# Router weights asked for earlier, and a new order of the work where attention passes into the experts

## The chip, the cores and the metric

One core of a Trainium2 chip runs the kernel. Its five engines (TensorE or PE for matmuls, VectorE or DVE, ScalarE or ACT, GpSimd or POOL, and SyncE or SP, which here only issues DMAs) each run their own list of instructions in order and meet at semaphores. The metric is the device time of one execution in microseconds (us).

## What is computed

16 batches of 256 tokens of width 256 go through a gated cross attention and a mixture of 8 experts, of which each token takes 2. Cut to what matters:

```python
q = layernorm(x)                                # per batch [256, 256]
K, V, Q = q @ wk, q @ wv, ctx @ wq              # the reference calls them so
attn = softmax(Q @ K.T, axis=2)
x = x + tanh(g_xattn) * (attn @ V)
xt = layernorm(x).reshape(4096, 256)
scores = xt @ Wg.T                              # 8 experts
top_scores, top_idx = top_k(scores, 2)
y_e = (silu(xt @ W1[e].T) * (xt @ W2[e].T)) @ W3[e].T     # hidden width 704
out = sum over the two chosen e of top_scores * y_e
x = x + tanh(g_ffn) * out
```

The function is called with the context as the query side: `_L0_xattn_ref(ctx_1024, _layernorm(x), ...)`; in the kernel x gives the rows of the result and the context gives what they attend to.

## The kernel before

**Attention, 16 steps.** Step n works on batch n. SP loads x(n) and the context. PE turns x (`turn_x`), multiplies (`product`, L823) and turns the probabilities (`turn_probs`); ACT takes the exponents (`exponents`, L673) and copies out of PSUM; DVE takes maxima, moments and the residual (`residual`, L1161 to L1169). The residual of batch n is made in step n + 1, after `values(n)` on PE. In the same steps the expert weights are cut in two f16 parts. ACT makes the high part (`high3`, L679, and the scaled copy at L725), DVE the low part (`lo12`, L1074, and `lo3`, L1081), with a scale worked out from sums of squares (L874, L1054, L1056). DVE takes the first moments of x(n + 2) ahead of the scale of step n (`first_moments`, L1100).

**Routing.** For a batch m whose residual is done, DVE takes `second_moments` (L1178), POOL makes the power -0.5 of the variance (`deviations`, L549 to L552, or `second_deviations`, L560 to L562), DVE chooses experts (`choose`, L1190 to L1214), PE counts ranks (`rank`, L837), DVE makes `slots` (L1138 to L1147), and POOL scatters the rows in four indirect DMAs (`scatter`, L572) into `rows_by_expert`. `AT_STEP` routes batches 0 to 9 in the steps, `AT_PAIR` batches 10 to 15 in pairs 0 to 5 of the expert stage. For batches 0 to 9 the normed rows are made on POOL (`low_rows`, L582 to L591), for the others on DVE and ACT (`centre_rows` L1112, `high_rows` L1122, `norm_rows` L658).

**Experts.** 32 pairs of tiles of 128 gathered rows, then 7 single tiles. For pair i, SP fetches rows (L502), PE turns them (`turn_gathered`, L866), ACT copies (`copy_turned`, L700), PE multiplies the gate part (36 matmuls, L946) and the upper part (30), ACT takes the silu (`gate`, L745 and L747), DVE multiplies (`mixed` L1380, `combined` L1386), ACT and DVE cut the result in two parts (`high` L756, `low` L1402 and L1403), PE makes the output (`to_output`, L978) one pair later, ACT scales it (L769), and POOL adds it into `out` (`add_rows`, L613). `units` (L1060 to L1228) prepares scales that `gate` needs.

**The order around the change.** All order is written out by hand: each engine runs its own function with a loop over steps and then one over pairs, and every instruction behind a wait stands with it. At the start, SP asks for wq, wk, context 0, x(0), wv and the first expert weights, and ACT asks for the router weights `wg_s` once wk is there. PE first sums the router weights (L884), then turns x(0). At step 15 ACT copies the first gathered rows before its high part, and PE turns them before `values(14)`. In pair 0 PE turns the last probabilities, makes `values(15)` and waits for the residual of batch 15 before the rank of batch 10; DVE makes that residual after choosing batch 10. POOL makes the power for batch 10 after the four scatters of batch 8.

## Time and profile before

| what | value |
|---|---|
| median of 3 runs | 597.12 us (595.77 to 597.38) |
| profiled execution, its own time | 590.55 us |
| its span, first to last instruction | 588.80 us |
| PE busy | 561.5 us, 95% |
| DVE, ACT, POOL busy | 322.2, 312.8, 290.4 us |
| mean granted clock of PE | 0.988 |
| attention steps and their seam to the experts | 0 to about 176 us |
| expert pairs and tiles | about 160 to 589 us |

A row of the timeline gives the start in us, the duration, the engine, the line, the operation with what it writes and reads, how many instructions are merged, and in brackets how long the engine had been idle and who released it. PEld is the load of weights into PE, SPq and ACTq are DMA issues. A granted clock of 1.00 is 2.4 GHz and 0.50 is 1.2 GHz.

### The profile page before, as it was taken

To read this page: it belongs to the slowest core of one execution; us is meant where nothing else is said; L and a number is where in the kernel's file an instruction comes from. 1 tells how busy PE (TensorE), PEld (TensorE's weight loads), DVE (VectorE), ACT (ScalarE), POOL (GpSimd) and SP (SyncE) were. 2 spreads that over 40 slices of the span, in tenths; PEclk is the share of its full clock that TensorE was granted. 3 is DMA by queue.
4 is the path that set the end of the run, shared out by engine and by line. 5 is a ranking of instruction groups with operands and counts; after the bars stand their busy time and mean duration, and the time that the engine had idled before them with its cause. 6 is when DMAs were issued, how large, how long until landed. Compare 5 with 4: busy or idle time off the path is not lost.

```text
span 588.8 us, 14558 instructions
## 1 busy us (share of the span) xinstructions
PE 561.5 (95%) x4641; PEld 489.8 (83%) x4641; DVE 322.2 (55%) x908; ACT 312.8 (53%) x438; POOL 290.4 (49%) x262
## 2 busy tenths in 40 slices
PE   6998999999779999899999999999999999999995
PEld 5787887787668999789988988988898899898883
DVE  2499898899877776843433343343334334333332
ACT  2787988788654555353534444354453444434442
POOL 3039898988984766643243333324323233333323
PEclk8999999999898999999999999999999999999999
DMA  7647879786413344532323323322232332322322
GB/s 252 191 156 213 256 258 291 210 278 182 159 69 122 77 85 114 162 65 49 56 39 47 66 40 47 54 51 41 47 65 39 47 63 42 47 40 43 53 35 27
DMA packets 52371, 61.49 MB, mean 104 GB/s; under 512 B 7632, under 2 KB 46160, under 8 KB 52304
## 3 DMA queue, kind: packets, MB, share of 16 engines
q1 hardware_dynamic: 34096, 38.14, 21.8%
q0 software_dynamic: 13296, 18.23, 18.2%
q10 hardware_dynamic: 4912, 4.20, 2.1%
q8 instruction: 45, 0.74, 0.5%
q14 instruction: 22, 0.18, 0.1%
HBM read 36.90 MB, written 23.66 MB: 103 GB/s over the span
## 4 chain that ended last, share of the span: by engine, by line
PE 71%; POOL 19%; issue 4%; DVE 2%; DMA 2%; ACT 1%; POOLq 0%; SPq 0%; DVEq 0%
PE psum L946 38%; PE psum L978 22%; POOL rows_by_expert L572 7%; POOL arena L582 5%; PE psum L955 4%; PE psum L866 3%; POOL rstd L552 2%; POOL xn2r L591 2%; PE psum L823 1%; POOL xn2r L588 1%; DMA wg_s<-in_WgT 1%; POOL var_eps L550 1%; PE psum L964 1%; DMA arena<-in_wkT 1%; POOL var_eps L549 0%
## 5 line engine op out<-in xcount | busy, mean ns | idle before, releaser
L613 POOL DMA_INDIRECT out<-w_in,id_s x71 | 129.5, 1823 | 235.0 <-ACT w_in L769 117.7
L946 PE MATMUL psum<-arena,w_hi 128*128 128x256 f16 x1408 | 213.2, 274 | 1.7 <-issue 1.7
L946 PEld LDWEIGHTS psum<-arena,w_hi 128*128 x1408 | 138.4, 98 | 19.1 <-issue 2.0
L946 PE MATMUL psum<-arena,w_lo 128*128 128x256 f16 x704 | 135.4, 274 | 0.0
L700 ACT ACTIVATE arena<-psum 128x1024 f16<-128x1024 f16 (+1 forms) x39 | 36.9, 947 | 106.0 <-PE psum L866 106.0
L1386 DVE SCALAR_TENSOR_TENSOR arena<-psum,h_unit,arena 128x1280 f32<-128x1280 f32 x32 | 49.6, 1551 | 64.7 <-PE psum L946 64.6
L572 POOL DMA_INDIRECT rows_by_expert<-xn2r,slot_i x64 | 72.1, 1127 | 18.2 <-issue 17.6
L946 PEld LDWEIGHTS psum<-arena,w_lo 128*128 x704 | 69.3, 98 | 8.4
L823 PE MATMUL psum<-arena 128*128 128x264 f32 x256 | 65.3, 401 | 3.5 <-DVE place L1138 3.2
L745 ACT ACTIVATE arena<-psum,w_unscale 64x256 f32<-64x256 f32 x32 | 15.0, 467 | 86.6 <-PE psum L946 86.6
L978 PE MATMUL psum<-w_hi,arena 128*128 x396 | 59.0, 273 | 1.0 <-ACT arena L759 1.0
L1380 DVE SCALAR_TENSOR_TENSOR arena<-psum,h_unit,arena 64x256 f32<-64x256 f32 x32 | 15.7, 490 | 77.2 <-ACT arena L747 77.0
L823 PEld LDWEIGHTS psum<-arena 128*128 128x128 f32 x256 | 47.3, 194 | 12.1 <-DVE halves L1054 4.0
L978 PE MATMUL psum<-w_hi,w_in 128*128 x385 | 57.3, 273 | 0.0
L747 ACT ACTIVATE arena<-psum,w_unscale 128x1280 f32<-128x1280 f32 x32 | 42.5, 1327 | 0.4
L978 PEld LDWEIGHTS psum<-w_hi,arena 128*128 128x128 f16 x396 | 37.8, 98 | 5.5 <-issue 1.2
L769 ACT ACTIVATE w_in<-psum,wsum 128x256 f32<-128x256 f32 x71 | 33.1, 467 | 14.5 <-PE psum L978 14.5
L978 PEld LDWEIGHTS psum<-w_hi,w_in 128*128 128x128 f16 x385 | 36.8, 98 | 4.1
L978 PE MATMUL psum<-w_lo,arena 128*128 x216 | 33.5, 272 | 0.0
L978 PE MATMUL psum<-w_lo,w_in 128*128 x210 | 32.5, 273 | 0.0
L823 PE MATMUL psum<-wv_s,arena 128*128 128x264 f32 x128 | 31.2, 387 | 0.3 <-ACT wv_s L711 0.3
L823 PE MATMUL psum<-arena,qk 128*128 128x256 f32 x128 | 30.9, 385 | 0.0
(195 smaller groups left out, 860.8 us busy)
## 6 DMA issues: line engine op xcount, KB each, us to landing
xa<-rows_by_expert SPq DMA_DIRECT2D x71, 136.0 KB, 2.2
w_in<-in_W1T SPq DMA_DIRECT2D x8, 704.0 KB, 5.4
w_in<-in_W2T SPq DMA_DIRECT2D x8, 640.0 KB, 5.0
w_in<-in_W3T SPq DMA_DIRECT2D x8, 640.0 KB, 5.9
arena<-in_ctxT SPq DMA_DIRECT2D x16, 256.0 KB, 6.1
xa<-in_x SPq DMA_DIRECT2D x16, 256.0 KB, 6.3
out<-xa ACTq DMA_DIRECT2D x16, 256.0 KB, 4.7
out<-w_in,id_s POOLq DMA_INDIRECT x71, 4.5
```

Of the source, the lines that this page charges most:

```text
L572: pool.indirect_dma_start(out=xs[:, :], out_offset=bass.IndirectOffsetOnAxis(ap=slot_i[:, k, col:col + 1], axis=0), in_=xn2r[:, m % ROWS, ...
L582: ins = pool.tensor_scalar(xn2f[:, t, :], xa[:, x_at(m) + t, :], mv2[:, m % 2, t, 0:1], rstd[:, half_of(m), t:t + 1], ALU.subtract, ALU.mult)
L613: pool.indirect_dma_start(out=out[:, :], out_offset=bass.IndirectOffsetOnAxis(ap=id_s[:, t8:t8 + 1], axis=0), in_=y_s[:, t8 % 4, :], in_of ...
L700: act.activation(xg_t[:, k, :, :, 0:n], xt_ps[:, :, :, 0:n], ACT.Copy).then_inc(s_xgt, 1)
L747: act.activation(act_g[:, 0:KF * N2], g_ps, ACT.Silu, scale=w_unscale[:, 0, bass.ds(expert[u], 1)].bitcast(F32)).then_inc(s_silu, 1)
L769: act.activation(y_s[:, t8 % 4, :], y_ps[t8 % 2], ACT.Copy, scale=wsum[:, t8:t8 + 1]).then_inc(s_y_copied, 1)
L823: ins = pe.matmul(dst[:, t, :], left[:, c, t * P:(t + 1) * P], right[:, c, :], start=(c == 0), stop=(c == 1))
L866: ins = pe.transpose(xt_ps[:, h, c, half * P:(half + 1) * P], xg[:, k, half, at:at + P // 2].bitcast(F16), ident16[:])
L946: ins = pe.matmul(flat_ps[:, j * N2:(j + 1) * N2], w12[w_part][:, c, bass.ds(e * (2 * H) + j * P, P)], xg_t[:, k, x_part, c, :], start=(q ...
L955: ins = pe.matmul(dst, xg_t[:, k, x_part, c, 0:P], w12[w_part][:, c, bass.ds(e * (2 * H) + at, n)], start=(q == 0 and c == 0), stop=(q == ...
L978: ins = pe.matmul(y_ps[t8 % 2], hid_p[k4 % 2][:, c * n + h * P:c * n + (h + 1) * P], w3[w_part][:, r, bass.ds(e * D, D)], start=(q == 0), ...
L1386: dve.scalar_tensor_tensor(out=hid[:, 0:KF * N2], in0=u_ps, scalar=h_unit[:, 0, bass.ds(e, 1)].bitcast(F32), in1=act_g[:, 0:KF * N2], op0= ...
```

## The change

It has three parts. At the start, SP asks for the router weights as its third request; ACT waits for wq instead of wk and asks only for the two gates. At step 15, ACT copies the first gathered rows after its high parts and exponents, and makes the high part of the last W3 there; PE makes `values(14)` first, then turns the gathered rows and the last probabilities. In step 15 and pair 0, DVE makes `units` after the residual of batch 14, `mixed` and the residual of batch 15 ahead of the choice of batch 10, and the low part of the last W3 after `combined(0)`; POOL makes the power of batch 10 ahead of the scatters of batch 8, and that of batch 11 ahead of those of batch 9. No instruction is added or removed.

```diff
             sp.dma_start(wk_t, ...).then_inc(s_wk, 16)
+            sp.dma_start(wg_s[:], WgT.rearrange("(c p) e -> p c e", p=P)).then_inc(s_wg_in, 16)
             load_ctx(0)
...
                 if n in AT_STEP:
                     low_rows(AT_STEP[n])
+                if n == B - 1:
+                    second_deviations(IN_STEPS)
                 if n - 1 in AT_STEP:
                     scatter(AT_STEP[n - 1])
-            second_deviations(IN_STEPS)
...
             for i in range(SLOTS + 1):
+                if i + 1 in AT_PAIR:
+                    second_deviations(AT_PAIR[i + 1])
                 if i == 0:
                     scatter(IN_STEPS - 1)
-                if i + 1 in AT_PAIR:
-                    second_deviations(AT_PAIR[i + 1])
...
-            act.wait_ge(s_wk, 16)
-            act.dma_start(wg_s[:], ...).then_inc(s_wg_in, 16)
+            act.wait_ge(s_wq, 16)
...
                 if live(n - 2):
                     store_rows(n - 2)
-                if n == B - 1:
-                    copy_turned(0, 0)
                 if live(n):
...
-                if live(n) and k == 1 and n < B - 1:
+                if live(n) and k == 1:
                     high3(e)
+                if n == B - 1:
+                    copy_turned(0, 0)
...
                 if at == 0:
-                    high3(E - 1)
+                    copy_probs(B - 1)
                     act.activation(silu_first[:], tanh_g[:], ACT.Silu)
-                    copy_probs(B - 1)
                     act.wait_ge(s_unit, 1)
...
                 if k == 1:
                     weight_sum3(n // 2)
+                if live(n - 1):
+                    values(n - 1)
                 if n == B - 1:
                     pe.wait_ge(s_pt_copied, B - 1)
                     turn_gathered(0, 0, 0)
-                if live(n - 1):
-                    values(n - 1)
+                    turn_probs(B - 1)
...
                         if at == 0:
                             to_hidden(range(4), expert[u], k)
-                            turn_probs(B - 1)
                             pe.wait_ge(s_v_copied, B)
...
-                if n == B - 1:
-                    units()
                 if n in AT_STEP:
                     choose(AT_STEP[n])
...
+            units()
             second_moments(IN_STEPS)
-            lo3(E - 1)
...
+                if at == 0:
+                    mixed(i, expert[u])
+                    residual(B - 1)
                 if m is not None:
                     centre_rows(m)
                     high_rows(m)
                     choose(m)
                 if on(i):
-                    if pair(i):
+                    if pair(i) and at > 0:
                         mixed(i, expert[u])
                     weights_and_rows(i, j, k4, expert[u])
+                    combined(i, expert[u])
                     if at == 0:
-                        residual(B - 1)
-                    combined(i, expert[u])
+                        lo3(E - 1)
                     low(i, k)
```

## Rows read from the trace of the kernel before

**Rows 1.** The page, part 1: busy time, share of the span, instructions.
```profile
PE 561.5 (95%) x4641; PEld 489.8 (83%) x4641; DVE 322.2 (55%) x908; ACT 312.8 (53%) x438; POOL 290.4 (49%) x262
```
**Rows 2.** Chain that ended last, in order of time: start, us, what.
```profile
4.97 5.88 DMA wg_s<-in_WgT
...
176.51 9.94 PE psum L946 x66
...
188.81 3.93 PE psum L946 x36
...
245.85 1.70 issue
```
**Rows 3.** Timeline of the start, 0 to 24 us.
```profile
10.98 0.84 PE L884 MATMUL psum<-wg_s,ones_f 128*128 128x8 f32 x4 [3.29 <-DMA wg_s<-in_WgT]
...
17.94 0.75 DVE L1100 BATCH_NORM_STATS2 stats<-xa 128x6 f32<-128x256 f32 x2 [2.65 <-DMA xa<-in_x]
...
19.63 1.46 ACT L725 ACTIVATE w_hi<-w_in,w_scale 128x1408 f16<-128x1408 f32 x1
...
21.96 0.56 ACT L673 ACTIVATE arena<-psum,nbias,rstd 128x256 f32<-128x256 f32 x1 [0.87 <-DVE nbias L1157]
```
**Rows 4.** Timeline of the seam, 150 to 180 us: PE and ACT.
```profile
157.92 1.01 PE L866 MATMUL psum<-ident,xa 128*128 128x128 f16 x8 [3.01 <-DMA xa<-rows_by_expert]
...
158.73 3.29 PE L823 MATMUL psum<-arena 128*128 128x264 f32 x8
...
158.97 1.02 ACT L700 ACTIVATE arena<-psum 128x1024 f16<-128x1024 f16 x1 [4.49 <-PE psum L866]
...
162.33 1.57 ACT L679 ACTIVATE w_hi<-w_in,w_scale 128x1536 f16<-128x1536 f32 x1
...
176.29 0.19 PE L837 MATMUL psum<-mask,before 128*128 128x16 bf16 x1 [3.90 <-DVE xa L1169]
```
**Rows 5.** Stretches: us, busy of PE, PEld, DVE, ACT, POOL, clock, DMA share, GB/s.
```profile
11.00:13.00 2.00, 2.00 (x11) 2.00 (x12) 0.24 (x2) 0.19 (x1) 0.00 (x0) 0.54 0.59 192
...
178.00:180.00 2.00, 2.00 (x11) 1.40 (x10) 0.75 (x2) 1.21 (x1) 0.00 (x0) 0.50 0.93 298
...
190.00:300.00 110.00, 108.31 (x1036) 97.26 (x1034) 64.87 (x192) 52.02 (x66) 59.48 (x45) 1.00 0.39 84
```
**Rows 6.** DMA queues, 5 to 11 us: packets, MB, share of 16 engines.
```profile
q1 hardware_dynamic: 1475, 1.79, 89.7%
q10 hardware_dynamic: 392, 0.01, 3.6%
```
**Rows 7.** Timeline of the seam, 150 to 186 us: DVE.
```profile
156.23 0.40 DVE L1060 TENSOR_SCALAR w_unscale<-halves 128x16 int32<-128x16 int32 x2
...
157.33 1.22 DVE L1228 SCALAR_TENSOR_TENSOR unscale_y<-unscale_y,tanh_g,h_unit 128x8 f32<-128x8 f32 x1
...
161.38 2.02 DVE L1074 SCALAR_TENSOR_TENSOR w_lo<-w_in,w_scale,w_hi 128x704 f16<-128x704 f32 x2 [1.30 <-ACT w_hi L725]
...
164.57 0.74 DVE L1178 BATCH_NORM_STATS2 stats<-xa 128x6 f32<-128x256 f32 x2
...
171.79 0.16 DVE L1112 SCALAR_TENSOR_TENSOR shift<-mv,rstd 128x2 f32<-128x2 f32 x1 [3.00 <-POOL rstd L562]
...
174.17 0.49 DVE L1380 SCALAR_TENSOR_TENSOR arena<-psum,h_unit,arena 64x256 f32<-64x256 f32 x1
...
176.15 1.54 DVE L1386 SCALAR_TENSOR_TENSOR arena<-psum,h_unit,arena 128x1280 f32<-128x1280 f32 x1
...
179.24 0.42 DVE L1402 TENSOR_TENSOR arena<-arena 64x256 f16<-64x256 f32 x1 [1.55 <-ACT arena L756]
179.67 1.49 DVE L1403 TENSOR_TENSOR arena<-arena 128x1280 f16<-128x1280 f32 x1
...
185.11 0.36 DVE L1210 SCALAR_TENSOR_TENSOR xn2r<-arena,rstd,mask 128x8 f32<-128x8 f32 x2
```
**Rows 8.** Waits of DVE, 176 to 255 us: us in total, times, longest.
```profile
DVE arena L1386 <- PE psum L946: 5.9, 5, 2.4
```

More of the change, by code:

```diff
@@ L634, in _ @@
         def _(act):
-            act.wait_ge(s_wk, 16)
-            act.dma_start(wg_s[:], WgT.rearrange("(c p) e -> p c e", p=P)).then_inc(s_wg_in, 16)
+            act.wait_ge(s_wq, 16)
             with nc.allow_non_contiguous_dma(reason="one gate to every partition"):
```

## Prediction, made before the changed kernel was run

> **What bounds the kernel now.** I read the page first: TensorE (PE) is busy 95% of the span [rows 1]. That is an average over three stages, so the second view is the chain of waits in order of time. From 176.51 us on it is PE alone, pair after pair, with one gap of 1.70 us at 245.85 [rows 2]. Work that the change leaves as it is fills that stage, so the stage gets shorter only if it begins earlier. The question is how much earlier PE gets into it, and whether a wait grows inside it. The third view is the timeline of the two places where the change acts: the start, and the seam from 154 to 177 us between the last attention batches and the first expert pairs. At the start PE sits idle 3.29 us until the router weights land at about 10.9 us [rows 3]. At the seam it idles 3.01 us until the first gathered rows land (157.9), and 3.90 us until the residual of batch 15 is written (176.3) [rows 4]. The fourth view is the table by stretch: the granted clock is 0.54 in 11 to 13 us and 0.50 in 178 to 180, its lower level of 1.2 GHz, right after the idles of 3.29 and 3.90 us, and 1.00 from 190 to 300 [rows 5]. At 158 the slow values after the third idle show the same. What that costs is seen in the chain: 66 matmuls from 176.51 took 9.94 us, while 36 of the same kind took 3.93 us at the upper level (2.4 GHz) [rows 2], so 66 would take 7.2.
>
> Below, times are those of the profile of before; I first work out the seam as if it began at its old time, then add the start.
>
> **Part 1, router weights third on SP's queue.** The request moves from 4.97 us on ACT's queue to about 1.8 us, behind two loads. The sum L884 could then start when the q-k product ends, 10.98 less the idle 3.29, so at 7.7: PE leads by 3.3 us, and with no idle there is no reason for the fall of the clock either. But the next end is near. At batch 0 DVE takes the moments of x(2) before it makes the scale that ACT waits for, and it waited 2.65 us for x(2) to land at 17.9 [rows 3]. Those moments take until about 19.0 whatever PE does (0.75 and a short second instruction); the scale's two small instructions follow in some 0.35, so ACT's first high part (1.46 us, at 19.63) can start at 19.35 and end at 20.8. There the exponents of batch 0 start, which before came at 21.96 because the scores came late [rows 3]. So **1.1 us** of the 3.3 reach ACT, which is the dense engine of the next steps. All later loads are issued on semaphores of this work, so I let 1.1 us pass through to the seam.
> What it costs: one more issue on SP ahead of the first context, x(0) and value weights. The 256 rows of 32 bytes are small packets: in 5 to 11 us the queue of ACT moved 392 of them in 3.6% of 16 engines' 6 us, which is 9 ns each, where the 1475 packets of SP's queue took 58 ns each [rows 6]. So 256 take 256 x 9 / 16 = 0.14 us, and did so before as well. If each were as dear as a large one it would be 0.93 us, x(2) would land that much later and the 1.1 would be 0.2. I take 1.1, since the 9 ns are of the same transfer.
> The Trainium skill (DMA: Bandwidth & Descriptors, "Issuing engines are not separate DMA queues") says that the queues of all issuing engines end on the same 16 DMA engines and that spreading requests only saves issue time. By that rule the queue itself gives nothing, and only the 3.1 us earlier request counts; the landing 5.9 us after the issue, behind seven loads, agrees [rows 2]. The same page (Specifications) says that transfers below 512 bytes are slowed by a read-modify-write; by it the upper cost would be the likely one; the 9 ns of this trace speak against it.
>
> **Part 2, order at batch 15 on PE and ACT.** Before, ACT stood 4.49 us on the turn of gathered rows (L700 at 158.97) in front of the high part of batch 15, and PE stood in front of the values of batch 14, which then ran 3.29 us at the low clock [rows 4]. After: PE runs the values at once, 154.9 to 156.9 (3.29 at the low clock; between half of it, 1.65, and that; I take 2.0, as four such take 1.0), and idles about 1 us to 157.9, not 3. Then the turn (8 transposes) and the probabilities of batch 15 (4) at the upper level: done at 159.1. ACT: high part 154.75 to 156.2 (1.46, as in [rows 3]), exponents (two of 0.56 there) to 157.3, high part of W3 1.57 to 158.9 [rows 4], then the copy of the turned rows 158.9 to 159.9. That is the same end as before (158.97 + 1.02), so ACT's 4.1 us of work go into its wait at no cost. PE's first expert matmul starts at 159.9 instead of 161.64, where it stood behind the slow values.
> The gate part of pair 0 is 36 matmuls, 3.93: 164.0 (0.1 more for the rank). The values of batch 15 (two halves of about 1.0) end at 166.1 at the earliest.
>
> **Part 3, order on DVE.** Five spans between rows of DVE [rows 7] give the pieces: units 156.23 to 158.55 = 2.32; choice of batch 9, 158.55 to 160.08 (161.38 less its wait of 1.30) = 1.53; low part and residual 14, 161.38 to 164.57 = 3.19; centre, high rows and choice of batch 10, 171.79 to 174.17 = 2.38; mixed, weights and residual 15, 174.17 to 176.15 = 1.98. After: choice from 156.2 to 157.8, low part and residual 14 to 160.95 (its high part was ready at 156.2), units to 163.3, moments of batch 10 (about 0.95) to 164.2, slots 0.5, moments 11 to 165.7. ACT's gate starts at 164.05, when PE is done, and takes 1.8; units at 163.3 are in time by 0.7 us, which is their cover. Then mixed and residual 15 end at **167.6**, where before they ended at 176.15. PE no longer waits for them: its upper part of pair 0, 30 matmuls at 3.93 / 36, runs 166.1 to 169.5.
> Late next is the choice of batch 10, which now stands behind the residual: 167.6 + 2.38 = 170.0. The rank of batch 10 on PE waits for it, and so does the product u times gate (L1386), at 170.4 instead of 176.15. PE turns pair 1 by 170.1, ACT copies it in 1.02, and pair 1 starts at 171.2, not 176.49: **5.3 us**. PE's idle pieces are now 0.9, 0.8, 1.0 us; the 1.70 us of [rows 2] did not lower the clock [rows 5]. So 66 matmuls take 7.2, not 9.94, and PE leads by 8.0 at 178.4.
> Then DVE is late. The low part of W3 (1.8 us; L679 on ACT took 1.57 for the same tile) is put into the 1.55 us that DVE waits for ACT's high part [rows 7], so it costs 0.3 there: pair 0's low part ends at 175.7 (before 179.67 + 1.49 = 181.16). From that end to the weighted rows of batch 11 it took 185.11 + 0.36 - 181.16 = 4.3 [rows 7]: 180.0. PE reaches the rank of batch 11 at 178.9 and waits 1.1. Pair 2 starts about 1.9 after the rank, at 182.0, against 188.7 in [rows 2]: **6.5 us** (0.2 off for small issues). From there DVE waits for PE again in every pair (five times, 5.9 us in all, before this product [rows 8]), so it doesn't fall behind; the 1.70 at 245.85 stands behind DVE's planning of the later slots, which starts from PE's own product, so it stays.
>
> **Part 4, POOL.** The power of batch 10 goes in front of four scatters. DVE waited 3.00 us for it until 171.79 [rows 7]. Now POOL reaches it at 164.4 and the moments are there at 164.2, so it is ready at 165.4, and 167.6 needs it: 2 us of cover. The scatters of batches 8 and 9 move back 1.1 each (two powers of that size ahead of them); batch 9's end at about 177.3, as before. Queued behind are the power of batch 12 (needed at 188), scatter 10 and the first add, which needs pair 0's product only at 182.6. SP's gathers of pair 8 need all scatters 60 us later. So nothing here.
>
> **Sum.** 1.1 + 6.5 = 7.6 us. The profiled execution took 590.55 (span 588.80) and would take 583.0. The median of the runs shown is 597.12, 6.6 above the profiled one; I carry the difference over whole: 597.12 - 7.6 = **589.5**. As PE's clock differs from run to run, an error in that carry is likelier than one in the profile.
>
> **Rivals.**
> A, the whole wait at the start counts: 3.3 us and about 1.6 of low clock pass on, total 11.4, 585.7. For it: the weights' transfer is 5.88 us of the chain. Against: x(2), above. 0.05.
> B, the start gives nothing, since x(2) lands later: total 6.5, or 5.6 if everything behind slides: 590.6 to 591.5. 0.17.
> C, the clock falls once more. Three idles of 1 us lie within 14 us. At half rate from 171 on, pair 1 takes 9.9 again, but the 1.1 of waiting for DVE goes: 2.7 - 1.1 = 1.6 lost, or 3.3 if it happens at 158 too (less what DVE hides): 591 to 593. The Trainium skill (TensorE: Matmul & The Clock Gate, Part 1) says the clock follows how busy PE has been, so several short idles could add up to one long; by that rule C would be the forecast, at 591.1; the trace has no such cluster. 0.15.
> D, DVE takes the place of the waits: units or the values of batch 15 come later than I think and the choice of batch 10 holds rank, product and pair 1. For each microsecond one is lost; at 4 it is 593.5, at 7 nothing is left. 0.06.
> E, slower: PE stays at 1.2 GHz from 158 through 185, since its work is spread thinner, never idle long but never dense. Before, it was low for about 10 us of that stretch; 17 more cost 8.4 us, against 3.8 saved idle and 1.1: 597.12 + 3.5 = 600.6. It turns slower once the low time exceeds the old by 10 us. Against: 66 dense matmuls alone brought the level back. 0.03.
> F, the change doesn't do what it says: POOL's chain, unchanged up to 164, sets the seam, and PE's idle only moves from the residual to the choice of batch 10. Then some clock and 1 us are gained: 595 to 597. Against: the power of batch 10 leaves the queue of scatters. 0.05.
>
> **How the numbers follow.** The forecast has 0.49. The range is 586.5 to 594.0: below it A, above it E, F and the end of D; the lower end is the forecast with the 1.1 of waiting gone and x(2) 2 us earlier. Faster by over 0.3% (1.8 us, about what a measurement can tell from none): 0.91. Within: 0.05. Slower: 0.04.
>
> **What would show it.** In the profile after: L884 at about 7.7; the first L673 at 20.9; clock 1.00 in 11 to 13; the first L946 near 158.8 (159.9 less 1.1); no wait of PE on L1169; pair 1 at 170.1, and a wait of about 1 us at the second L837 of the expert phase, released by DVE's L1210. The exponents at 21 or later say B; clock 0.50 past 158 says C; a long wait of PE on DVE's choice says D or F.

## The result: faster by 1 to 4.5 us, where 7.6 were predicted

| comparison | before | changed | ratio, 95% interval |
|---|---|---|---|
| first | 596.43 us (594.88 to 602.7, 19 runs) | 594.4 us (592.24 to 598.21, 19 runs) | 0.9957 [0.9937, 0.9977] |
| second (`after_again`) | 590.52 us (24 runs) | 586.0 us (7 runs) | 0.9933 [0.991, 0.9957] |
| third (`after_third`) | 596.42 us (33 runs) | 595.34 us (10 runs) | 0.9969 [0.9943, 0.9995] |

The changed kernel is faster. The 594.4 us lie just above the range (586.5 to 594.0), and the gain in that comparison is 2.0 to 2.6 us. Medians are taken over all runs of a kernel and ratios over its fast runs alone (one run of `before_again` took 2064 us), so the two can differ a little. The kernel before itself took 590 us in two comparisons and 596 in four; a section below shows what differs between these. The readings of the change are taken from traces of the first kind, where ACT has no pause of unknown cause: `before_again` (the kernel before, span 589.4), the trace shown ahead of the prediction (span 588.80), and `after_again` (the changed kernel, span 584.0, its own time 585.78). Between these spans the gain is 4.8 or 5.4 us, between the medians of that comparison 4.5.

Profile of the changed kernel (`after_again`), the page, part 1: busy time, share, instructions. PE is busy 559.6 us, not 561.5; with the shorter span its share went up by a point, and so did those of PEld and ACT [rows 1].

```profile
span 584.0 us, 14559 instructions
PE 559.6 (96%) x4641; PEld 488.3 (84%) x4641; DVE 322.8 (55%) x908; ACT 312.9 (54%) x438; POOL 290.7 (50%) x262
```

Its start, rows of the timeline; they answer [rows 3].

```profile
7.79 0.51 PE L884 MATMUL psum<-wg_s,ones_f 128*128 128x8 f32 x4
...
12.14 1.38 ACT L688 ACTIVATE w_hi<-w_in 128x1408 bf16<-128x1408 f32 x1 [2.71 <-DMA w_in<-in_W1T]
...
14.45 3.89 PE L823 MATMUL psum<-wv_s,arena 128*128 128x264 f32 x8 [2.70 <-ACT wv_s L712]
...
19.21 0.75 DVE L1100 BATCH_NORM_STATS2 stats<-xa 128x6 f32<-128x256 f32 x2 [4.76 <-DMA xa<-in_x]
...
20.52 1.47 ACT L724 ACTIVATE w_hi<-w_in,w_scale 128x1408 f16<-128x1408 f32 x1 [1.44 <-DVE w_scale L1056]
...
22.14 0.56 ACT L674 ACTIVATE arena<-psum,nbias,rstd 128x256 f32<-128x256 f32 x1 [0.16 <-DVE nbias L1157]
```

PE's wait of 3.29 us for the router weights is gone. In its place PE waits 2.70 us at 14.45 for the value weights from ACT, and ACT had waited 2.71 us for the first expert weights (W1) to land at 12.1. PE's granted clock is 0.50 from 13.1 to 19.9 us. DVE waits 4.76 us for x(2), which lands at 19.2 instead of 17.9, and ACT's first exponents start at 22.14 instead of 21.96.

PE at the seam, rows of the timeline of `after_again`; they answer [rows 4] and the chain in [rows 2].

```profile
158.06 0.61 PE L866 MATMUL psum<-ident,xa 128*128 128x128 f16 x8 [1.05 <-DMA xa<-rows_by_expert]
...
160.12 0.61 PE L947 MATMUL psum<-arena,w_hi 128*128 128x256 f16 x4 [1.01 <-ACT arena L701]
...
166.53 1.13 PE L823 MATMUL psum<-arena 128*128 128x264 f32 x4 [1.38 <-DVE place L1138]
...
171.97 0.17 PE L837 MATMUL psum<-mask,before 128*128 128x16 bf16 x1 [0.58 <-DVE xn2r L1210]
...
172.69 0.61 PE L947 MATMUL psum<-arena,w_hi 128*128 128x256 f16 x4 [0.53 <-ACT arena L701]
...
181.66 0.18 PE L837 MATMUL psum<-mask,before 128*128 128x16 bf16 x1 [1.15 <-DVE xn2r L1210]
...
183.89 0.60 PE L947 MATMUL psum<-arena,w_hi 128*128 128x256 f16 x4
```

The idles of 3.01 and 3.90 us have become 1.05 and 0.58. A new one of 1.38 stands at 166.5, behind DVE. The granted clock stays up; table by stretch (us; busy time of PE, PEld, DVE, ACT, POOL; clock; DMA share; GB/s), against [rows 5]:

```profile
11.00:13.00 2.00, 0.75 (x7) 0.66 (x6) 0.00 (x0) 0.86 (x1) 0.00 (x0) 1.00 0.96 329
178.00:180.00 2.00, 2.00 (x21) 1.80 (x20) 1.97 (x9) 1.20 (x2) 1.48 (x4) 1.00 0.24 85
```

DVE and POOL at the seam, `after_again`, rows of the timeline of each (against [rows 7]):

```profile
157.06 0.45 DVE L1197 TENSOR_TENSOR hot<-idx,iota_e 128x32 f32<-128x32 uint32 x1
...
157.76 1.01 DVE L1206 TENSOR_TENSOR seen<-seen,mask 128x8 bf16<-128x8 bf16 x1
...
163.05 1.00 DVE L1227 TENSOR_TENSOR unscale_y<-w_unscale 128x8 f32<-128x8 f32 x1
...
166.22 0.17 DVE L1138 TENSOR_TENSOR place<-psum,region_of 128x16 f32<-128x16 f32 x1 [0.95 <-issue]
...
172.09 1.54 DVE L1384 SCALAR_TENSOR_TENSOR arena<-psum,h_unit,arena 128x1280 f32<-128x1280 f32 x1
...
156.86 0.61 POOL L589 CAST xn2r<-arena 128x512 f16<-128x512 f32 x1
...
157.57 1.18 POOL L592 TENSOR_TENSOR xn2r<-arena,xn2r 128x512 f16<-128x512 f32 x1
...
162.88 1.15 POOL L592 TENSOR_TENSOR xn2r<-arena,xn2r 128x512 f16<-128x512 f32 x1
```

Three instructions of DVE that take 0.16 to 0.19 us elsewhere took 0.45, 1.01 and 1.00, and each ended within 0.04 us of the end of a POOL instruction that had begun before it: 157.51 against 157.47, 158.77 against 158.75, 164.05 against 164.03. And DVE idles 0.95 us from 165.3 on with no releaser. From 150 us to the rank of batch 11 at 181.66, the chain of waits of this trace is DVE's alone; the idle is in it as these pieces (start, us, what; L397 loads the number of an expert into a register):

```profile
165.10 0.16 DVEq L395
165.26 0.72 issue
165.98 0.19 DVEq L397
```

### The profile page after: what moved, and what is told of

Its sections match the earlier page's. It is cut to its first block, busy times and chain, and to the rows that moved or that the text cites. A ratio compares the mean times of both kernels' runs of the same rounds, so it can differ in the third digit from the quotient of the medians.

```text
span 596.5 us, 14559 instructions
## 1 busy us (share of the span) xinstructions
PE 564.6 (95%) x4641; PEld 489.2 (82%) x4641; DVE 322.6 (54%) x908; ACT 312.9 (52%) x438; POOL 292.2 (49%) x262
## 3 DMA queue, kind: packets, MB, share of 16 engines
q0 software_dynamic: 13296, 18.23, 17.9%
## 4 chain that ended last, share of the span: by engine, by line
PE 72%; DVE 15%; issue 4%; ACT 4%; SPq 2%; DMA 1%; another core or an unknown queue 1%; POOLq 0%; ACTq 0%; DVEq 0%
PE psum L947 38%; PE psum L979 22%; PE psum L956 4%; PE psum L823 4%; DVE w_lo L1074 3%; PE psum L866 3%; DVE xa L1169 1%; DMA xa<-in_x 1%; DVE stats L1100 1%; DVE w_lo L1081 1%; DVE stats L1178 1%; DVE nmax L1153 1%; PE psum L965 1%; ACT w_hi L688 1%
## 5 line engine op out<-in xcount | busy, mean ns | idle before, releaser
L947 PE MATMUL psum<-arena,w_hi 128*128 128x256 f16 x1408 | 215.0, 276 | 7.5 <-ACT arena L701 6.6
L947 PEld LDWEIGHTS psum<-arena,w_hi 128*128 x1408 | 138.9, 99 | 26.1 <-issue 8.7
L947 PE MATMUL psum<-arena,w_lo 128*128 128x256 f16 x704 | 135.9, 275 | 0.7 <-issue 0.7
L1384 DVE SCALAR_TENSOR_TENSOR arena<-psum,h_unit,arena 128x1280 f32<-128x1280 f32 x32 | 49.6, 1551 | 69.2 <-PE psum L947 66.8
L573 POOL DMA_INDIRECT rows_by_expert<-xn2r,slot_i x64 | 74.1, 1157 | 18.2 <-issue 17.9
L947 PEld LDWEIGHTS psum<-arena,w_lo 128*128 x704 | 69.5, 99 | 9.8 <-issue 1.2
L823 PE MATMUL psum<-arena 128*128 128x264 f32 x256 | 64.1, 396 | 3.8 <-DVE place L1138 3.5
L823 PEld LDWEIGHTS psum<-arena 128*128 128x128 f32 x256 | 46.3, 190 | 12.1 <-DVE halves L1054 3.5
L724 ACT ACTIVATE w_hi<-w_in,w_scale 128x1408 f16<-128x1408 f32 x16 | 23.5, 1469 | 15.7 <-DVE w_scale L1056 15.6
```

The costliest lines, as they stand in the source:

```text
L573: pool.indirect_dma_start(out=xs[:, :], out_offset=bass.IndirectOffsetOnAxis(ap=slot_i[:, k, col:col + 1], axis=0), in_=xn2r[:, m % ROWS, ...
L724: act.activation(w12[0][:, :, n * H:(n + 1) * H], w12_in[:, k], ACT.Copy, scale=w_scale[:, 0:1].bitcast(F32)).then_inc(s_hi12, 1)
L823: ins = pe.matmul(dst[:, t, :], left[:, c, t * P:(t + 1) * P], right[:, c, :], start=(c == 0), stop=(c == 1))
L947: ins = pe.matmul(flat_ps[:, j * N2:(j + 1) * N2], w12[w_part][:, c, bass.ds(e * (2 * H) + j * P, P)], xg_t[:, k, x_part, c, :], start=(q ...
L1384: dve.scalar_tensor_tensor(out=hid[:, 0:KF * N2], in0=u_ps, scalar=h_unit[:, 0, bass.ds(e, 1)].bitcast(F32), in1=act_g[:, 0:KF * N2], op0= ...
```

## Experiments

To compare traces whose start differs, I use two figures: the time at which ACT's first exponents start (**start**), and the time from DVE's maximum over the scores of batch 15 (L1153) to the first product of u and gate (L1386, in the changed kernel L1384) (**seam**). Kernel before: seam 21.01 and 20.70; changed: 16.75.

### Start and seam apart

`start_only` takes this from the change and nothing else:

```diff
             sp.dma_start(wk_t, wkT.rearrange("(c p) d -> p c d", p=P)).then_inc(s_wk, 16)
+            sp.dma_start(wg_s[:], WgT.rearrange("(c p) e -> p c e", p=P)).then_inc(s_wg_in, 16)
             load_ctx(0)
...
-            act.wait_ge(s_wk, 16)
-            act.dma_start(wg_s[:], WgT.rearrange("(c p) e -> p c e", p=P)).then_inc(s_wg_in, 16)
+            act.wait_ge(s_wq, 16)
```

`seam_only` is the rest of the change. `before_again` and `after_again` are the two kernels once more.

> The kernel before, unchanged, for a second trace beside the others of this group. Its first trace spanned 588.8 us, while its runs lie at 595 to 600. If that trace was an unusually undisturbed execution, this one spans 592 to 597 and shows idle pieces of 2 to 6 us in the expert pairs that the first did not have; if those pieces in the trace of the changed kernel belong to the change, this one has none of them. Ratio to the kernel before: 1.000.

> The changed kernel, unchanged, for a second trace. Its first trace had ACT idle for 4.7 us before the copy of the turned rows of pair 2 (186.9 us), and PE idle 3.3 us behind that, then a lower clock. If this belongs to the new order, it is there again at the same instruction and pair 2 starts near 188; if it is a disturbance of that one execution, pair 2 starts near 183.5 (about 5 us ahead of the kernel before). Ratio 0.995 to 0.997.

> Part 1 alone: the router weights are asked for third on SP's queue, everything else as before. Theory 1 (the load of x(2) ends the wait, and it lands later than before): exponents of batch 0 within 0.3 us of before, ratio 1.000 +- 0.002. Theory 2 (my prediction's 1.1 us, hidden in the trace by chance): exponents at 20.9 us, ratio 0.998. Theory 3 (the small rows delay the value weights, as seen in one trace, where they landed at 10.4 instead of 7.3 us): the value weights land after 10 us again.

> Parts 2 to 4 alone: the router weights are asked for by ACT as before, the order of step 15 and of pair 0 is the new one. Theory 1 (the gain of the change comes from the seam alone): the same time as the whole change, ratio 0.995 to 0.997, the product of pair 0 near 172.4 us. Theory 2 (the seam's gain is what I predicted, 6.5 us, and the start takes part of it back): ratio 0.989 to 0.992.

| kernel | median | ratio | x(2) at DVE | start | seam |
|---|---|---|---|---|---|
| before_again | 590.68 | 0.9995 [0.9979, 1.0011] | 17.25 | 23.67 | 20.70 |
| start_only | 589.77 | 0.9992 [0.9978, 1.0005] | 19.65 | 22.53 | 20.68 |
| seam_only | 587.17 | 0.995 [0.993, 0.9969] | 18.25 | 22.02 | 16.76 |
| after_again | 586.0 | 0.9933 [0.991, 0.9957] | 19.21 | 22.14 | 16.75 |

The start alone can't be told from no change; the seam alone is nearly the whole. The pause of 4.7 us in the first trace of the changed kernel is not in `after_again`, where pair 2 starts at 183.89; so it does not come with the new order by itself. In `before_again` PE's granted clock was at its lower level from 10.7 to 17.5 us and its exponents came at 23.67. `start_only` and `after_again` show the lower level too, from 13.1 to 19.9, about the wait for ACT's value weights (3.40 and 2.70 us). Of the nine traces with the start of the change, six have a low stretch between 13 and 21 us, with one such wait of 2.6 to 3.6 us; in the other three the waiting is split in pieces of 2.2 us and less, and the clock stays at 1.00. So what the earlier weights save of low clock, PE mostly pays a little later.

### What holds the start

> The changed kernel with the router weights asked for by ACT as its very first instruction, not by SP as its third. Theory 1 (the small rows in SP's queue push x(2) back, which landed at 19.1 to 19.7 us in three traces with them and at 17.3 to 18.3 in three without): the sum of the router weights starts at 7.5 to 7.9, x(2) lands by 18.3 and the exponents of batch 0 start at 21.0 to 21.3, 1 us ahead of the changed kernel's 22.1; ratio to the kernel before 0.991 to 0.992. Theory 2 (x(2) is late because all loads share the same bandwidth and PE, being ahead, asks for context 2 sooner): x(2) lands after 19 us again, ratio 0.993.

> The changed kernel with x(2) asked for ahead of the second batch of weights W2 and W3 instead of behind them. Theory 1 (the first exponents now wait for x(2), which lands at 19.0 to 19.7 us in five traces of the changed start): x(2) lands before 15 us, and the exponents of batch 0 start at 20.6 to 21.2 instead of 21.7 to 22.9; median 0.7 to 1.3 us under the changed kernel. Theory 2 (PE's own work and its clock set the first exponents, x(2) is only the last to be seen): still 21.7 or later, median as the changed kernel's or up to 1 us above it, since W2 and W3 land later.

> As combo, but x(2) is asked for behind the second weights, as in the changed kernel. Theory 1 (x(2) holds the start up also when wg is out of SP's queue): x(2) lands at 18.2 to 18.7, first exponents at 20.9 to 21.3, 0.4 to 0.8 us behind combo. Theory 2: no difference to combo.

> The changed kernel with three edits: ACT asks for wg in its first instruction, x(2) is asked for ahead of the second weights, and DVE loads the numbers of the first eight experts behind the low halves of batch 15. Theory 1 (they are three separate waits): x(2) lands by 15 us, the first exponents start at 20.3 to 20.8, the seam takes 15.9 to 16.3; 2.0 to 3.0 us under the changed kernel on the same chip. Theory 2 (PE's work sets the first exponents once x(2) is there, at 21.0): the start gives 1.0 at most, the whole 1.5 to 2.0.

wg_act_first, against the changed kernel:

```diff
-            sp.dma_start(wg_s[:], WgT.rearrange("(c p) e -> p c e", p=P)).then_inc(s_wg_in, 16)
             load_ctx(0)
...
         def _(act):
+            act.dma_start(wg_s[:], WgT.rearrange("(c p) e -> p c e", p=P)).then_inc(s_wg_in, 16)
             act.wait_ge(s_wq, 16)
```

x2_early, against the changed kernel:

```diff
             load_ctx(1)
+            load_x(2)
             load_w12(1)
             load_w3(0)
-            load_x(2)
```

`combo` has both and the early register load (below); `start_combo` is combo without the early x(2). First the rows of x2_early, then of combo (timelines of DVE and ACT):

```profile
15.86 0.75 DVE L1100 BATCH_NORM_STATS2 stats<-xa 128x6 f32<-128x256 f32 x2 [0.46 <-DMA xa<-in_x]
21.04 0.56 ACT L674 ACTIVATE arena<-psum,nbias,rstd 128x256 f32<-128x256 f32 x1 [0.87 <-DVE nbias L1157]
```

```profile
13.89 0.75 DVE L1100 BATCH_NORM_STATS2 stats<-xa 128x6 f32<-128x256 f32 x2 [0.17 <-DMA xa<-in_x]
20.09 0.56 ACT L674 ACTIVATE arena<-psum,nbias,rstd 128x256 f32<-128x256 f32 x1 [0.87 <-DVE nbias L1157]
```

| start as in | first exponents, every trace |
|---|---|
| the kernel before | 21.96, 22.02, 23.61, 23.67 |
| the change | 21.35, 21.71, 21.78, 21.80, 22.14, 22.53, 22.79, 22.87, 22.92 |
| the change, wg by ACT at once (x(2) late) | 21.12, 21.43 |
| the change, x(2) early | 21.04 |
| both | 20.09, 20.39, 20.75, 20.78 |

x2_early had been expected to bring x(2) before 15 us; it was 15.86, but the exponents came where expected. Medians: wg_act_first 584.62 (before 590.11 there), 0.9911 [0.9894, 0.9929]; x2_early 591.27 (before 595.7), 0.9934 [0.9896, 0.9973]. So both waits were real: from the mean of the nine (22.2) the one edit moves the exponents by 0.9 us, the other by 1.2, both together by 1.7. These are figures of the traces; the medians of these comparisons don't tell 1 us apart. The four traces with the start of before have a mean of 22.8, so the change's start is 0.6 ahead on average, with values that overlap. With the change's own start, x(2) was seen by DVE at 18.7 to 19.7 in nine traces; with the start of before, at 17.3 to 18.3 in four. SP's issues of the loads ahead of it took longer (3.06 us for the last two of W3 in `after_again`, 1.33 in the trace of before) and it was issued at 10.7 to 12.4 us in the nine traces, against 8.5 to 10.2 in the four of the old start. In four traces with the router weights in SP's queue PE also waits for the value weights, which land at 9.7 to 11.9 us (theory 3 of start_only); start_only itself does not show that wait. With the router weights asked for by ACT at once x(2) was issued at 10.0 and 10.4, and DVE saw it at 18.45 and 18.75.

The tables by stretch of before_again and of after_again, in that order, 5 to 10 us, show the DMA engines less full in the new start:

```profile
5.00:10.00 5.00, 1.97 (x8) 1.44 (x8) 1.31 (x6) 1.88 (x2) 0.84 (x3) 1.00 0.95 315
```

```profile
5.00:10.00 5.00, 4.77 (x30) 4.17 (x29) 2.52 (x9) 2.25 (x3) 0.98 (x3) 1.00 0.78 274
```

Why they are less full is not settled: the share is 0.83 in wg_act_first as well, where the small packets are not in SP's queue, so these packets alone are not it.

### Which engine's order makes the seam

Each of these leaves the order of one engine, or of PE and ACT, as before, or changes PE and ACT alone. The edits are the pieces of the change's diff for these engines, taken back or taken alone. That of pool_undone, against the changed kernel:

```diff
-                if n == B - 1:
-                    second_deviations(IN_STEPS)
                 if n - 1 in AT_STEP:
                     scatter(AT_STEP[n - 1])
+            second_deviations(IN_STEPS)
...
-                if i + 1 in AT_PAIR:
-                    second_deviations(AT_PAIR[i + 1])
                 if i == 0:
                     scatter(IN_STEPS - 1)
+                if i + 1 in AT_PAIR:
+                    second_deviations(AT_PAIR[i + 1])
```

> The changed kernel with DVE's whole order as before: units ahead of the choice of batch 9, the choice of batch 10 ahead of mixed and the residual of batch 15, the low part of W3 before pair 0. The orders of PE, ACT, POOL and the start are the new ones. Theory 1 (most of the seam's gain is PE no longer waiting for the residual): PE waits 2 us or more for L1169 again, ratio 0.996 to 0.998. Theory 2 (the gain is that of PE's and ACT's order at step 15): ratio 0.993 to 0.994.

> The changed kernel with POOL's part undone: the power for batch 10 after the four scatters of batch 8 again, that for batch 11 after those of batch 9. Theory 1 (this power must be ready when the residual of batch 15 is done, at 169.6): the power is ready at about 171 to 171.8, DVE waits 1.5 to 2.2 us for it, and the time rises by as much, ratio 0.996 to 0.997. Theory 2 (POOL's part has cover and is worth nothing): ratio 0.993.

> The kernel before with only the orders of PE and of ACT at the seam changed (value products ahead of the turn of gathered rows, the turn of the probabilities behind it, ACT's copies and the last squares in the order that this needs); start, DVE and POOL are as before. The time from the scores of batch 15 to the first combined step is 20.7 us in the kernel before, 16.75 in the changed one, 16.69 with DVE's order put back, 17.46 with POOL's put back. Theory 1 (PE's order makes the gain, DVE's order is worth nothing, POOL's 0.7): 17.3 to 17.6 us, so 3.1 to 3.4 us under the kernel before in the median. Theory 2 (each of the two is worth nothing only while the other is there): 18.5 us or more, the gain 2 us or less.

> The changed kernel with the orders of PE and of ACT at the seam as before; start, DVE and POOL are changed. Theory 1 (PE's order makes the gain): PE waits at its first turn of gathered rows about 3 us as before, and the seam takes 19.8 to 20.7 us, of which POOL's part takes at most 0.7; median within 1 us of the kernel before. Theory 2 (the wait of 3.9 us on the last residual is DVE's and POOL's to remove): the seam takes 18 us or less.

| order at the seam | median | before there | ratio | seam |
|---|---|---|---|---|
| all changed (after_again) | 586.0 | 590.52 | 0.9933 [0.991, 0.9957] | 16.75 |
| DVE as before | 585.6 | 590.11 | 0.9917 [0.9897, 0.9936] | 16.69 |
| POOL as before | 585.45 | 590.11 | 0.9929 [0.9909, 0.9948] | 17.46 |
| PE and ACT as before | 593.88 | 595.7 | 0.9952 [0.9917, 0.9986] | 18.12 |
| only PE and ACT changed | 595.79 | 595.7 | 1.0001 [0.9964, 1.0038] | 19.66 |
| nothing changed (before_again) | 590.68 | 590.52 | 0.9995 [0.9979, 1.0011] | 20.70 |

The changed seam takes 16.72 to 16.76 us in the three traces without pauses of ACT (after_again, seam_only, wg_act_first) and 17.2 to 17.4 in the three with them (the first trace, x2_early, after_third). The two rows of PE and ACT are of the second kind, so between them and the others only steps of 1 us and more count; the 0.7 of POOL is between traces of the first kind. The expectations missed more than once. dve_undone was to wait 2 us or more for L1169 or be worth as much as PE's order alone; PE waits 0.92 and the time is that of the change. pool_undone was to rise by 1.5 to 2.2 us; DVE waits 0.56 and the median does not rise. The two rows of PE and ACT came out against theory 1: with these alone it said 17.3 to 17.6, and it is 19.66; with these undone 19.8 to 20.7, and it is 18.12. Theory 2 of pe_act_only holds: the parts are not a sum. Rows of the timeline that say why, of pe_act_only (DVE, PE), where both old waits stand unchanged:

```profile
172.11 0.16 DVE L1111 SCALAR_TENSOR_TENSOR shift<-mv,rstd 128x2 f32<-128x2 f32 x1 [2.99 <-POOL rstd L562]
176.61 0.18 PE L836 MATMUL psum<-mask,before 128*128 128x16 bf16 x1 [3.90 <-DVE xa L1168]
```

of pool_undone (DVE):

```profile
168.72 0.16 DVE L1111 SCALAR_TENSOR_TENSOR shift<-mv,rstd 128x2 f32<-128x2 f32 x1 [0.56 <-POOL rstd L563]
```

of dve_undone (PE, DVE):

```profile
173.03 0.18 PE L837 MATMUL psum<-mask,before 128*128 128x16 bf16 x1 [0.92 <-DVE xa L1169]
158.39 1.23 DVE L1228 SCALAR_TENSOR_TENSOR unscale_y<-unscale_y,tanh_g,h_unit 128x8 f32<-128x8 f32 x1
```

The wait of 3.90 us for the residual comes from DVE's wait of 3 us for POOL's power of batch 10. Two edits remove that: POOL makes the power before its scatters, or DVE does the residual before it asks for the power. With PE and ACT changed, DVE's edit alone takes the seam from 19.66 to 17.46 and POOL's alone to 16.69; POOL's on top of DVE's adds 0.7, DVE's on top of POOL's nothing. And the new order of PE and ACT is worth 1.0 alone and up to 1.4 on top of the others.

Why is DVE's order worth nothing once POOL's is changed? Add its pieces up, from the instruction behind the last w_scale (L1056) to the first product: 15.69 us in after_again (156.40 to 172.09), 15.60 in dve_undone (157.29 to 172.89). The change takes the low half of W3 out (1.70), exposes the register load that it had hidden (0.95), and puts choice and units at moments at which POOL's instructions stretch them more: 2.64 + 1.99 = 4.63 against 1.54 + 2.25 = 3.79, so 0.84. 0.95 + 0.84 - 1.70 = +0.09.

### The two costs on DVE, each taken away

`regs_early` loads the eight numbers behind the low halves of batch 15, `pool_quiet` lets POOL compute the low rows of batches 8 and 9 on 8 of 256 columns; it leaves out the others, so its result is not the function's and it serves for the timing alone.

regs_early:

```diff
                 if n == B - 1:
                     lo12(n)
+                    held = [dve.alloc_register(f"expert_{u}") for u in range(UNROLL)]
+                    expert = {}
+                    dve.wait_ge(s_map, 1)
+                    take_experts(dve, held, expert, 0, UNROLL)
                 if live(n - 1):
                     residual(n - 1)
...
-            held = [dve.alloc_register(f"expert_{u}") for u in range(UNROLL)]
-            expert = {}
...
-            dve.wait_ge(s_map, 1)
-            over_slots(dve, moe_step, lambda i, n: take_experts(dve, held, expert, i, n))
+            over_slots(dve, moe_step, lambda i, n: take_experts(dve, held, expert, i, n) if i > 0 else None)
```

pool_quiet, the first of its three instructions (the cast and the subtraction are cut in the same way):

```diff
+                w = 8 if m in (8, 9) else D
                 for t in range(KT):
-                    ins = pool.tensor_scalar(xn2f[:, t, :], xa[:, x_at(m) + t, :], mv2[:, m % 2, t, 0:1],
+                    ins = pool.tensor_scalar(xn2f[:, t, 0:w], xa[:, x_at(m) + t, 0:w], mv2[:, m % 2, t, 0:1],
```

> The changed kernel with DVE's load of the experts of pairs 0 to 7 into registers put right behind the low part of batch 15, where DVE is busy, and not between the moments of batch 10 and the slots of batch 9. Theory 1 (the idle 0.95 us before L1138 in the trace of the changed kernel is this load, and PE's 1.38 us wait for L1138 is mostly it): the idle piece is gone, PE's wait for L1138 is 0.4 to 0.5, the product of pair 0 starts 0.9 us earlier at about 171.2, ratio 0.9915 to 0.992. Theory 2 (DVE waits there for PE's rank of batch 9): nothing moves, ratio 0.993.

> The changed kernel in which POOL computes the low rows of batches 8 and 9 on 8 of 256 columns (the other columns keep older values), so that POOL's operations of 0.6 to 3.3 us beside the choice of batch 9 and the units are nearly gone. Theory 1 (DVE's small operations are stretched by POOL's that run beside them): the choice of batch 9 takes 1.5 to 1.6 us instead of 2.64, the units 1.1 to 1.3 instead of 1.99, PE's wait of 1.38 us for the places is gone, and the seam takes 15.0 to 15.5 us instead of 16.75; median 1.2 to 1.7 us under the changed kernel. Theory 2 (the stretch has to do with the operations themselves or with DMA): choice 2.6, units 2.0, time as the changed kernel's.

regs_early: 583.42 us, 0.990 [0.9882, 0.9918], seam 15.91. PE's wait for the places is 0.38 instead of 1.38 (timeline, PE):

```profile
163.71 1.13 PE L823 MATMUL psum<-arena 128*128 128x264 f32 x4 [0.38 <-DVE place L1138]
```

pool_quiet: 590.5 us (before 595.7), 0.9877 [0.9813, 0.994], seam 16.38; timeline, DVE:

```profile
156.56 0.19 DVE L1198 TENSOR_TENSOR hot<-idx,iota_e 128x32 f32<-128x32 uint32 x1
...
157.00 0.17 DVE L1207 TENSOR_TENSOR seen<-seen,mask 128x8 bf16<-128x8 bf16 x1
...
160.82 0.17 DVE L1228 TENSOR_TENSOR unscale_y<-w_unscale 128x8 f32<-128x8 f32 x1
...
164.11 0.17 DVE L1139 TENSOR_TENSOR place<-psum,region_of 128x16 f32<-128x16 f32 x1 [1.92 <-PE psum L839]
```

The stretch is POOL's: all three instructions are back at 0.17 to 0.19, the choice takes 1.54 (155.89 to 157.43; expected 1.5 to 1.6) and the units 0.77. That is 2.3 us less for DVE, but the seam became only 0.4 shorter: DVE now waits 1.92 for PE, whose gathered rows came 3.9 us after the scores instead of 2.7. The expected 15.0 to 15.5 missed that next floor. So that POOL's work stretches these instructions is shown. What the stretch alone costs the seam is not: the run moved the gathered rows too, and why they came later is open.

The Trainium skill (SBUF — State Buffer, "Who interferes with whom") says just this: a DVE instruction with two inputs in SBUF and a POOL instruction that reads SBUF share a port pair, and the one that comes second is blocked until the first ends. The three ends above agree with it to 0.04 us. They are ends of POOL's cast (L589) and of its subtraction (L592). Beside POOL's L583, which reads SBUF as well and ran from 153.53 to 156.79, the same trace does not show it: DVE's L1141 at 155.01 took 0.19 us and L1157 at 156.06 took 0.16, both with two inputs.

### The best version

> The changed kernel once more, beside the three below on one chip: 4.0 to 5.0 us under the kernel before; first exponents at 21.7 to 22.9 us, seam (scores of batch 15 to the first combined step) 16.7 to 17.3.

> ACT asks for wg first and x(2) is early, as in combo, but DVE keeps the order of the kernel before at the seam (units ahead of the choice of batch 9, the last low half ahead of the first combined step, where it hides the register load). Theory 1 (DVE's new order takes 1.8 us of low half off the path and lays 0.9 of stretch and 0.95 of register load on it): seam 16.7, 0.6 to 0.9 us slower than combo. Theory 2 (the two orders are equal to PE): within 0.3 us of combo.

> combo once more. Theory 1 (the pause belongs to the chip and not to the order): where the kernel before is at 590, no pause of ACT over 3 us between 178 and 190, seam 15.9 to 16.3, 7 us under the kernel before; where the kernel before is at 596, 3 to 5 us under it. Theory 2 (the pause comes with this order of instructions): pause of 4 to 5 us, 2 us under the kernel before on any chip.

> combo_dve_old once more: no pause of ACT over 3 us, seam 16.7 on a chip where the kernel before is at 590, 5.5 to 6.5 us under it; 4 us under it where it is at 596.

| kernel | median | before there | ratio | start | seam |
|---|---|---|---|---|---|
| after_third | 595.34 | 596.42 | 0.9969 [0.9943, 0.9995] | 21.35 | 17.36 |
| combo | 595.64 | 596.42 | 0.9964 [0.9936, 0.9992] | 20.09 | 17.30 |
| start_combo | 596.11 | 596.42 | 0.9998 [0.9964, 1.0032] | 21.43 | 17.28 |
| combo_dve_old | 592.53 | 596.42 | 0.9938 [0.9905, 0.997] | 20.75 | 18.29 |
| combo_again | 593.05 | 596.29 | 0.994 [0.9917, 0.9962] | 20.78 | 17.10 |
| combo_dve_old_again | 591.29 | 596.29 | 0.9913 [0.9892, 0.9933] | 20.39 | 17.78 |

combo was expected 2 to 3 us ahead of the changed kernel and came level with it (595.64 and 595.34). In these six traces DVE idles 0.44 to 1.47 us just before its product, put down to "remote" (see below). Without that idle the seam is 15.8, 15.9 and 16.6 in the three with the early register load (combo, combo_again, start_combo), 16.9 in after_third, 17.1 and 16.8 in the two of combo_dve_old: something of the 0.8 us of the early register load is there, but the medians don't show it. DVE's old order was expected 0.6 to 0.9 us behind combo, or within 0.3; both times it was ahead in the median, by 3.1 and 1.8 us, though its seam is the longer one. after_third was expected 4 to 5 us under the kernel before and is 1.1 under it; combo_again is 3.2 under it, as theory 1 has it for such a chip, and combo_dve_old_again 5.0, but with pauses of ACT of up to 7.1 us where none over 3 was expected. The runs of either pair overlap, so which of DVE's orders is the better one stays open; `combo_dve_old` (changed start with both edits, PE, ACT and POOL as changed, DVE as before) is ahead of the changed kernel here, at 592.53 against 595.34, though the intervals overlap. regs_early and wg_act_first, at 0.990 and 0.9911, stand against the changed kernel's 0.9933 of a neighbouring comparison.

### Where the kernel before takes 590 us and where 596

No run was made for this; it was read from twenty traces, and none of them is of the kernel before where it takes 596. In the nine traces whose kernel before was (or itself took) 590 us, ACT has no idle time between 165 and 262 us that the profile puts down to "remote" (no instruction of this core released it). In each of the eleven others it has four to eight of them, up to 9.0 us long. The first trace of the changed kernel (own time 598.21), and after_third, ACT:

```profile
186.91 1.02 ACT L701 ACTIVATE arena<-psum 128x1024 f16<-128x1024 f16 x1 [4.74 <-remote]
...
244.77 0.47 ACT L746 ACTIVATE arena<-psum,w_unscale 64x256 f32<-64x256 f32 x1 [5.78 <-remote]
```

```profile
185.27 1.02 ACT L701 ACTIVATE arena<-psum 128x1024 f16<-128x1024 f16 x1 [4.83 <-remote]
```

In after_third ACT ends its work at 180.4, PE has finished turning the rows that it needs by about 181.2, and ACT starts on them at 185.27; PE idles 3.39 us for it and the clock of 180 to 200 falls to 0.83. From the second product of u to the third it took 16.9 us there, 10.7 in after_again. pe_act_only, nearest to the kernel before, has no pause of that size between 165 and 200, only at 217.8 and 250. So where the kernel before takes 596, the changed kernel may pay for a pause that the kernel before is spared. That would fit its gain of 1.1 to 2.0 us there against 4.5 where no pause is, but it is not shown.

The semaphores tell one thing more. Each trace also keeps the times at which semaphores were updated. At 186.91 in the first trace ACT waits for the semaphore that PE's last turn updates: the row of that turn ends at 182.98, and the update comes at 186.89, 3.9 us later. In the nine traces without pauses every update by PE between 160 and 262 us comes within 0.04 us of the end of its row; in each of the eleven others 9 to 15 of some 45 come 0.3 to 7.4 us after it. Every idle of ACT and DVE in this stretch that is put down to "remote" ends with an update by PE, and updates by ACT itself don't come late. So the engine that is late is PE, or its rows stand too early in these stretches, and ACT and DVE wait for it. Why PE is late stays open; no kernel was made to tell.

## Why the prediction missed

By its own steps, with after_again; its seam began 0.2 us later than that of the trace ahead of the prediction.

| step | predicted | measured |
|---|---|---|
| L884 can start | 7.7 | 7.79 |
| x(2) lands no later | 17.9 | 19.21 |
| exponents of batch 0 | 20.8 | 22.14 |
| first expert product | 159.9 | 160.12 |
| choice of batch 9 | 1.53 us | 2.64 us |
| low part and residual 14 | 3.19 us | 3.21 us |
| units | 2.32 us | 1.99 us |
| places (L1138) on DVE | 164.2 | 166.22 |
| residual 15 ends | 167.6 | 169.6 |
| wait of PE on L1169 | gone | gone |
| pair 1 starts | 171.2 | 172.69 |
| 66 matmuls of pair 1 | 7.2 us | 7.2 us |
| wait for the rank of batch 11 | 1.1 us | 1.15 us |
| pair 2 (first L947) | 182.0 | 183.89 |

**Start, 1.1 predicted, nothing measurable.** The step that failed is "those moments take until about 19.0 whatever PE does": x(2)'s landing was taken as fixed, and it moved back by over 1 us with the start's order of loads. That was rival B. I had weighed the 256 small packets at 0.14 to 0.93 us and looked at their time in the queue, not at when SP could issue what stands behind. A second step failed as well: "with no idle there is no reason for the fall of the clock either". PE met the next idle, 2.70 us at 14.45, behind ACT's wait for W1, and the clock was at its lower level from 13.1 to 19.9.

**Seam, 6.5 predicted, 4.8 measured** (188.7 to 183.89), or 5.0 with the later beginning. The mechanism was right: no wait on the residual, full clock, DVE's lateness at the rank of batch 11 to 0.05 us. Two terms were mis-sized. "Choice 1.53" is a price read where POOL happened not to interfere; started at 156.40 instead of 158.55 it met two POOL instructions and took 2.64. And "moments 0.95, slots 0.5" left out the load of eight registers that the low half of W3 had hidden: of that step I had asked what it costs at its new place, not what it covered at its old one. 1.1 + 0.95 less 0.33 for the units is 1.7 of the 1.5 to 1.7 missing. For part 4 I had found "nothing here"; it is 0.7 with DVE's new order, and up to 3.0 without it. These 0.7 are inside the 4.8, so they are not a part of what is missing.

**Rivals.** D had the right sign of cause (DVE takes the place of the waits) at 0.06, far too little; it came true at 1.7 us, and it is D and B together that the clean traces show. C did not happen in them: the three idles of 1.05, 1.01 and 1.38 us left the clock at 1.00 from 156 to 200. In six of the eleven traces with ACT's pauses it did, at 170.4 to 173.5 us: in the first trace, that of the comparison the prediction is held against, the clock is 0.50 from 173.5 to 176.9 and again low from 187.1 to 194.0. The rule of the Trainium skill (TensorE: Matmul & The Clock Gate, Part 1), by which C would have been the forecast, thus gave no loss in the clean traces, where the idles stayed at 1.4 us and below.

**The carry.** "I carry the difference over whole", 6.6 us between the profiled execution and the median, named as the likeliest error, was wrong in kind: the difference is not a property of the kernel, since the kernel before took 590 in one comparison and 596 in another. Where it is absent the changed kernel took 586.0 (583.0 would be the profile's own sum); where it is present the gain shrinks. In the first comparison this is about half of the miss: of 7.6 us predicted 4.5 to 4.8 are there without pauses, and 2.0 with them. Why the rest goes stays open; the first trace shows pair 2 at 188.2 us, behind the pause at 186.9, where after_again has 183.89.

## What to carry to other kernels

When an order is changed, list what the moved instruction was covering (here a register load of 0.95 us) and what will run beside it at its new place; a DVE instruction with two SBUF inputs can be held until the POOL instruction beside it ends, as these traces show for a cast and a subtraction. Edits on several engines that remove one and the same wait are substitutes, not a sum: ask of each what is left if the other is there. A load moved ahead can move all behind it in its queue, so the next landing on each engine's path is the term to compute (here x(2) for DVE and W1 for ACT), not the one that is brought forward. And before a chain is put down to the engine that waits, look at when the semaphore it waits for was updated.

## What the runs showed of the hardware

DVE's short instructions took 0.16 to 0.19 us alone and 0.45 to 1.01 beside a POOL cast or subtraction begun before them. This makes the same code run in different lengths: batches 11 to 15 of the attention took 36.44 us in after_again and 34.98 in regs_early, which are the same up to there. The difference begins in batch 12: from the start of L1141 to the start of L1214, behind the two L1210, DVE needs 4.4 us in the one (127.62 to 132.03) and 3.0 in the other (127.09 to 130.10). Two instructions of it on DVE and the one on POOL that held the second up, after_again:

```profile
127.62 0.52 DVE L1141 TENSOR_TENSOR placed<-hot,place 128x32 f32<-128x32 f32 x1
...
130.15 0.54 DVE L1203 TENSOR_TENSOR mask<-hot 128x16 bf16<-128x16 f32 x1
...
130.06 0.61 POOL L589 CAST xn2r<-arena 128x512 f16<-128x512 f32 x1
```

The same two of DVE in regs_early:

```profile
127.09 0.23 DVE L1141 TENSOR_TENSOR placed<-hot,place 128x32 f32<-128x32 f32 x1
...
129.15 0.18 DVE L1203 TENSOR_TENSOR mask<-hot 128x16 bf16<-128x16 f32 x1
```

L1203 ended at 130.69, L589 at 130.67, in the one; in the other L589 began after L1203 was done. The largest piece is the first L1210: 1.14 us in the one, ending at 131.95 beside POOL's L592, which ended at 131.92, and 0.22 in the other. Why L1141 differs is not explained by this: POOL's L583 had begun 0.06 us before it in both, and the rule of the ports would hold it to the end of L583 at 128.79, where it ended at 128.14. A small shift between two engines thus decides over 1.4 us, and a difference of that size between two kernels is no proof of an edit by itself.
